# A decoder layer on one core: batches outside heads, every weight part kept on chip, and a batch's later layers woven into the next batch's heads through one PSUM bank

## The chip, the cores and the metric

The kernel runs on one core of a Trainium2 chip. The metric is the device time of one execution in microseconds (us), from start to end; lower is better. Three runs of the kernel before gave 434.12, 434.87 and 435.01 us. The engines are TensorE (PE; its weight loads are listed as PEld), VectorE (DVE), ScalarE (ACT), GpSimd (POOL) and SyncE (SP), which here issues the DMAs. SBUF is the on-chip memory of 128 partitions, PSUM the eight banks (512 fp32 for each partition) that TensorE writes.

## The reference

There are 4 batches of 256 tokens with 256 channels, 16 heads of width 128. In short:

```
# L0_attn: 16 heads, head width 128
q, k, v = x @ Wq, x @ Wk, x @ Wv              # 256 -> 16 x 128 each
q, k = rmsnorm(q) * q_rms_w, rmsnorm(k) * k_rms_w
scores = q k^T / sqrt(128) - slope[h] * distance, causal
y = rmsnorm(softmax(scores) @ v) * subln_w
x = layernorm(x + concat(y) @ Wproj)           # Wproj 2048 x 256
# L0_xattn: attention computed from ctx alone, applied along x's channel axis
a = softmax((ctx Wq'^T + bq)(ctx Wk'^T + bk)^T)
x = layernorm(x + x @ a^T)
# L0_ffn: weights rounded to three levels, activations to 8 bits
h = sigmoid(quant(x) @ quant(Wgate)^T) * (quant(x) @ quant(Wup)^T)
out = layernorm(x + quant(h) @ quant(Wdown)^T)
```

## The kernel before

**Instruction streams.** Every engine runs one list of instructions in order; the lists are written out by hand, with semaphores between them. Nothing reorders them, so an instruction that waits holds back all that stands behind it on its engine.

**Heads first, batches inside.** The attention is 64 *steps*, each one head of one batch. `attention_steps` (L206) runs over heads outside and over the 4 batches inside; eight steps (two heads) make one trip of a hardware loop. The pipeline is deep: in step `n` TensorE projects q, k and v of step `n` (`qkv(0)`, `qkv(1)`, one for each 128 tokens, L470 to L484, six matmuls of 384 columns each), turns the normed q and k of step `n-1` (L493), turns the probabilities of step `n-2` (L499), computes the scores of `n-1` (L505, L506) and the values of `n-2` (L512 to L514), and turns y of `n-3` (L521). The fp32 inputs are split into a high and a low part, and three products of the parts are summed.

**Who does what in a step.** ScalarE takes squares of q and k and copies v (L635, L639), applies the exponential (L644, L645), copies qT, kT and yT (L661, L662, L651) and squares y (L673). VectorE sums the squares (L797, L804), norms q and k (L791) and y (L812), copies the turned probabilities out of PSUM (L817) and adds the bias to the scores with a running extreme (L835). GpSimd computes the reciprocal roots by a power (L310, L315), splits the weights of the next head into parts (L276, L280) and halves the bias (L325). The order that matters below is VectorE's: `norm` of tile 1 of the step before, y's sum, `sums(0)`, y's norm, the copy pT, `norm(0)`, `sums(1)`, the scores.

TensorE may not overwrite q, k, v of a tile until that tile is normed, and may not turn q and k before both tiles are normed:

```
qkv(0)
if live(1):
    for t in range(TT):
        pe.wait_ge(s_qkn[t], n)
    ...
    last.then_inc(s_tqk, 1)
...
qkv(1)
```

**Weights.** Two heads' parts are on chip at a time; SyncE loads the next head while one is used, three DMAs for each. The feed-forward weights are rounded and turned in the last three steps of each trip (`quantise_ff`, `turn_ff`), 24 pieces of 256 columns. The cross attention of all four batches is computed ahead of the heads and in their first steps.

**After the heads.** yT of all 64 steps lies in SBUF. A loop over the 8 tiles of 128 tokens (L535 to L589) runs projection (`project`, L410), first layer norm, cross attention, second norm, gate, up, hidden quantisation, down and last norm. One tile's feed-forward half is woven with the next tile's first half, and the projection matmuls of later tiles (`fill`) stand in TensorE's gaps.

## Time and profile before

| what | value |
|---|---|
| median of three runs | 434.87 us |
| profiled execution: span from first to last instruction | 432.9 us |
| its time around the span, taken as the median less the span | 2.0 us |
| busy: PE, DVE, ACT, POOL | 401.9, 327.7, 254.4, 220.2 us |
| bytes moved | 14.52 MB |

An engine's busy time is the time in which at least one of its instructions runs. The profiled execution's own time is known only as its span; the whole time of a run is taken as the span plus 2.0 us. Clock means the TensorE clock that was granted, with 1.00 for full speed.

### The profile page before, as it was taken

Reading aid. Unit: us, or ns where it says so; the run is one execution under the profiler, and the core shown is the slowest. Engines: PE = TensorE matmul, PEld = TensorE weight load, DVE = VectorE, ACT = ScalarE, POOL = GpSimd, SP = SyncE. Lnnn points to the kernel's source line nnn. Section 1 sums busy time; section 2 is a strip of 40 time slices with the busy share of each in tenths; the row PEclk is TensorE's granted clock in tenths of the full one; section 3 lists DMA queues with packets and bytes.
Section 4 is the critical chain, followed back from the end, with each engine's and each line's share of the span. In section 5 each row is a group of like instructions: output and inputs, shape, how many; then the busy total and the mean of one; then the engine's idle time right before and its main releaser. Section 6 shows DMA issues by size and latency. Waiting matters only on the chain.

```text
span 432.9 us, 9595 instructions
## 1 busy us (share of the span) xinstructions
PE 401.9 (93%) x2605; PEld 361.1 (83%) x2612; DVE 327.7 (76%) x1000; ACT 254.4 (59%) x750; POOL 220.2 (51%) x368
## 2 busy tenths in 40 slices
PE   4979999999999999999999999999999899999552
PEld 3668899999999999999999999999988677777321
DVE  0777987887797798788779779878822788888862
ACT  3486777677676776767767677676722333333321
POOL 3633667676675776767767677675501122222210
PEclk9999999999999999999999999999999999999965
DMA  8980010110101101011010110000000000000000
GB/s 223 316 251 2 2 36 3 38 37 0 36 0 36 36 0 36 0 36 36 0 36 0 36 36 0 0 0 0 0 2 0 2 0 15 12 14 12 13 14 24
DMA packets 21747, 14.52 MB, mean 34 GB/s; under 512 B 1760, under 2 KB 21472, under 8 KB 21728
## 3 DMA queue, kind: packets, MB, share of 16 engines
q1 hardware_dynamic: 21728, 14.29, 11.2%
q8 instruction: 9, 0.15, 0.2%
q14 instruction: 10, 0.08, 0.1%
HBM read 13.24 MB, written 1.05 MB: 33 GB/s over the span
## 4 chain that ended last, share of the span: by engine, by line
PE 86%; DVE 5%; ACT 4%; issue 2%; DMA 1%; POOL 1%; SPq 0%; POOLq 0%; DVEq 0%
PE ps L482 30%; PE ps L422 11%; PE ps L493 7%; PE ps L506 6%; PE ps L499 5%; PE ps L512 4%; PE ps L505 3%; PE ps L514 3%; PE ps L513 3%; PE ps L521 3%; PE ps L587 3%; PE ps L572 2%; ACT hT L696 2%; DMA x_sb<-in_x 1%; PE ps L557 1%
## 5 line engine op out<-in xcount | busy, mean ns | idle before, releaser
L315 POOL TENSOR_TENSOR qk_rstd<-qk_sum,minus_half 128x2 f32<-128x2 f32 x128 | 88.5, 692 | 92.6 <-DVE qk_sum L797 90.8
L482 PE MATMUL ps<-w_hi,xT_hi 128*128 128x384 f32 x256 | 96.9, 378 | 2.3 <-DVE qk_n L791 1.4
L482 PE MATMUL ps<-w_hi,xT_lo 128*128 128x384 f32 x256 | 86.5, 338 | 0.0
L482 PE MATMUL ps<-w_lo,xT_hi 128*128 128x384 f32 x256 | 86.3, 337 | 0.0
L797 DVE TENSOR_REDUCE qk_sum<-sq 128x2 f32<-128x258 f32 x128 | 53.6, 419 | 30.8 <-ACT sq L635 29.1
L635 ACT ACTIVATE sq<-ps 128x256 f32<-128x256 f32 x128 | 49.1, 384 | 34.6 <-PE ps L482 34.4
L791 DVE TENSOR_TENSOR qk_n<-ps,qk_rstd 128x256 f32<-128x256 f32 x128 | 54.2, 423 | 18.8 <-POOL qk_rstd L315 17.8
L422 PE MATMUL ps<-wp,yT 128*128 128x256 f32 x256 | 62.2, 382 | 0.0
L310 POOL TENSOR_TENSOR y_rstd<-y_sum,minus_half 128x2 f32<-128x2 f32 x64 | 49.0, 766 | 24.6 <-DVE y_sum L804 20.9
L673 ACT ACTIVATE sqy<-ps 128x258 f32<-128x258 f32 x64 | 24.8, 387 | 58.5 <-PE ps L514 58.5
L422 PEld LDWEIGHTS ps<-wp,yT 128*128 128x128 f32 x256 | 46.7, 190 | 5.9
L482 PEld LDWEIGHTS ps<-w_hi,xT_hi 128*128 128x128 f32 x256 | 48.4, 189 | 3.0 <-DVE qk_n L791 1.7
L482 PEld LDWEIGHTS ps<-w_lo,xT_hi 128*128 128x128 f32 x256 | 48.6, 190 | 0.0
L482 PEld LDWEIGHTS ps<-w_hi,xT_lo 128*128 128x128 f32 x256 | 48.0, 188 | 0.0
L352 POOL TENSOR_SCALAR var_eps<-mean_var 128x1 f32<-128x1 f32 x24 | 7.0, 292 | 79.6 <-DVE mean_var L846 79.6
L835 DVE CUSTOM_DVE_ANT_0 score<-ps,bias 128x128 f32<-128x128 f32 (+1 forms) x128 | 40.3, 352 | 2.8 <-PE ps L506 2.8
L493 PE MATMUL ps<-ident,qk_n 128*128 128x128 f32 x256 | 38.7, 273 | 0.8 <-DVE qk_n L791 0.6
L506 PE MATMUL ps<-kT,qT 128*128 128x256 f32 x128 | 38.2, 380 | 0.0
L280 POOL TENSOR_TENSOR w_lo<-w_raw,w_hi 128x256 fp32r<-128x256 f32 x48 | 35.4, 738 | 4.0
L817 DVE COPY pT<-ps 128x384 f32<-128x384 f32 x64 | 35.1, 548 | 2.6 <-PE ps L499 2.5
L493 PEld LDWEIGHTS ps<-ident,qk_n 128*128 128x128 f32 x256 | 31.1, 140 | 5.0 <-issue 3.2
L639 ACT COPY v_sb<-ps 128x128 f32<-128x128 f32 x128 | 34.0, 266 | 0.0
(126 smaller groups left out, 846.9 us busy)
## 6 DMA issues: line engine op xcount, KB each, us to landing
w_raw<-in_L_attn_Wq SPq DMA_DIRECT2D x16, 128.0 KB, 2.2
w_raw<-in_L_attn_Wk SPq DMA_DIRECT2D x16, 128.0 KB, 2.3
w_raw<-in_L_attn_Wv SPq DMA_DIRECT2D x16, 128.0 KB, 2.3
wp<-in_L_attn_Wproj SPq DMA_DIRECT2D x1, 2048.0 KB, 16.1
ff_raw<-in_L_ffn_w_gate SPq DMA_DIRECT2D x1, 1024.0 KB, 8.6
ff_raw<-in_L_ffn_w_up SPq DMA_DIRECT2D x1, 1024.0 KB, 11.0
ff_raw<-in_L_ffn_w_down SPq DMA_DIRECT2D x1, 1024.0 KB, 13.0
out<-fin SPq DMA_DIRECT2D x8, 128.0 KB, 1.7
```

Source lines behind the costliest of these rows:

```text
L280: pool.tensor_tensor(lo, raw, hi, ALU.subtract).then_inc(s_split, 1)
L310: pool.tensor_tensor(y_rstd[:], y_sum[:], minus_half[:], ALU.pow).then_inc(s_ry, 1)
L315: pool.tensor_tensor(qk_rstd[:, t, :], qk_sum[:, t, :], minus_half[:], ALU.pow).then_inc(s_rs[t], 1)
L422: last = pe.matmul(ps[:, u % 2, 0:C], yT[:, h * B + b, t * P:(t + 1) * P], wp[:, h, :], start=(h == 0), stop=(h == H - 1))
L482: last = pe.matmul(ps[:, t, 0:3 * D], xa[:, k, tok], wa[:, r, k * 3 * D:(k + 1) * 3 * D], start=(i == 0), stop=(i == len(parts) - 1))
L493: last = pe.transpose(dst[:, t * P:(t + 1) * P], qk_n[:, t, a, :], ident[:])
L506: pe.matmul(ps_s[:, S1], qT[:, P:T], kT[:], start=True, stop=True).then_inc(s_s, 1)
L635: act.activation(sq[:, t, :, 0:D], ps[:, t, 0:2 * D].rearrange("p (a d) -> p a d", a=2), ACT.Square).then_inc(s_sq[t], 1)
L791: dve.tensor_tensor(qk_n[:, t], ps[:, t, 0:2 * D].rearrange("p (a d) -> p a d", a=2), r, ALU.mult).then_inc(s_qkn[t], 1)
L797: dve.tensor_reduce(qk_sum[:, t, :], sq[:, t], AX.X, ALU.add).then_inc(s_ss[t], 1)
L817: dve.tensor_copy(pT[:], ps_pT).then_inc(s_pT, 1)
L835: last = dve.tensor_tensor_reduce(score[:, s], ps_s[:, s], bias[:, r, s], 1.0, 3e38, ALU.add, ALU.min, neg_max[:, t:t + 1])
```

## The change

The kernel is rewritten around a different loop order.

- **Order.** Steps are `n = b * 16 + h`: a batch's 16 heads, then the next batch. The steps are no hardware loop any more but are written out. SBUF holds the high and low parts of all 16 heads (`w_hi`, `w_lo`); `w_lo` lies over the raw weights.
- **Splitting the weights.** `split_hi` is now a VectorE copy of 768 columns at the end of steps 0 to 12 (head `n+3`), and heads 1 and 2 before the first step; GpSimd computes only the low parts, three pieces in each of steps 0 to 13. The loads come in groups of heads (1, 1, 2, 4, 4, 4), six DMAs each.
- **Projection.** Each head is multiplied with `Wproj` in step `n+4` (`project(n - 4)`), accumulated in one bank for the whole batch.
- **Turned probabilities** (pT) are copied by ScalarE instead of VectorE. qT and kT share a bank with the scores, so turning q and k of the next head waits for the scores to be read.
- **Side bank.** All other TensorE work goes through one bank, in two slots a step: slot 0 between turning the probabilities and `qkv(n, 1)`, slot 1 after the values. Each job waits until the job before it has been read.
- **Later layers.** Batches 0 to 2 run their projection's end, both norms, cross attention and feed-forward in the 17 steps of the next batch; batch 3 runs them after the last step, both tiles side by side. The sigmoid is replaced by a tanh, `sigmoid(z) = (1 + tanh(z/2)) / 2`.
- **Feed-forward weights** are quantised in 6 units of 1024 columns, in VectorE's steps 7, 9, 11, 13, 15, 17.

The diff, cut to its core:

```diff
+    for b in range(B):
+        first = b * H + (2 if b == 0 else 1)
+        slots[first, 0] = ("ctx_turn", b)
+        slots[first + 1, 0] = ("ctx_project", b)
+        slots[first + 2, 0] = ("energies", b)
+        slots[first + 3, 1] = ("attn_turn", b)
+        if b < LAST:
+            slots[b * H + (13 if b == 0 else 7), 1] = ("x_turn", b + 1)
+            n = b * H + H
+            slots[n + 5, 1] = ("x1_turn", b)
+            slots[n + 6, 1] = ("cross", b)
+            slots[n + 9, 0] = ("xq_turn", b)
+            for i in range(4):
+                slots[n + 9 + i, 1] = ("gate", b, i)
+                slots[n + 10 + i, 0] = ("up", b, i)
+            slots[n + 14, 0] = ("hq_turn", b, 0)
+            slots[n + 15, 1] = ("hq_turn", b, 1)
+            slots[n + 16, 0] = ("down", b)
+    slots[7, 0] = ("ff_sums",)
+    FF_STEPS = [8, 10, 12, 14, 16, 18]
+    for i, n in enumerate(FF_STEPS):
+        slots[n, 1] = ("ff_turn", i)
...
         @block.sync
+            load_x(0)
+            load_w(0)
+            load_w(1)
+            for n, v in ((0, q_rms), (1, k_rms), (2, subln), (3, xbq), (4, xbk)):
+                sp.dma_start(vecs[:, n:n + 1], v.rearrange("(p a) -> p a", a=1)).then_inc(s_vec, 16)
+            load_w(2)
+            sp.dma_start(xw_sb[:, 0, :], xwq).then_inc(s_xw, 16)
+            sp.dma_start(xw_sb[:, 1, :], xwk).then_inc(s_xw, 16)
+            load_ctx(0)
+            load_wp(0)
+            load_w(3)
+            load_ff(0)
...
         @block.gpsimd
+            for n in range(STEPS + 3):
+                s, b = n % H, n // H - 1
+                if n >= 3:
+                    pool.wait_ge(s_ssy, n - 2)
+                    wait(pool, s_yn, n - 3)
+                    pool.tensor_tensor(y_rstd[:], y_sum[:], minus_half[:], ALU.pow).then_inc(s_ry, 1)
+                if n + 2 < H:
+                    split_lo(n + 2, 0)
+                if n < STEPS:
+                    for t in range(TT):
+                        pool.wait_ge(s_ss[t], n + 1)
+                        wait(pool, s_qkn[t], n)
+                        pool.tensor_tensor(qk_rstd[:, t, :], qk_sum[:, t, :], minus_half[:], ALU.pow).then_inc(s_rs[t], 1)
+                        if n + 2 < H:
+                            split_lo(n + 2, t + 1)
...
         @block.tensor
+            def turn_qk(n):
+                for t in range(TT):
+                    pe.wait_ge(s_qkn[t], n + 1)
+                wait(pe, s_sc, n)
...
+            def project(n):
+                b, h = divmod(n, H)
+                pe.wait_ge(s_yT, n + 1)
...
+                for t in range(TT):
+                    last = pe.matmul(total[:, t * C:(t + 1) * C], yT[:, n % 2, t * P:(t + 1) * P], wp[:, h, :],
+                                     start=(h == 0 and t == 0), stop=(h == H - 1), skip_group_check=True)
+                last.then_inc(s_pr, 1)
...
+            for n in range(STEPS + DEPTH):
+                if n < STEPS:
+                    qkv(n, 0)
+                if 0 <= n - 1 < STEPS:
+                    turn_qk(n - 1)
+                if 0 <= n - 2 < STEPS:
+                    turn_p(n - 2)
...
+                slot(n, 0)
+                if n < STEPS:
+                    qkv(n, 1)
+                if 0 <= n - 1 < STEPS:
+                    scores(n - 1)
+                if 0 <= n - 2 < STEPS:
+                    values(n - 2)
+                slot(n, 1)
+                if 0 <= n - 4:
+                    project(n - 4)
+                if 0 <= n - 3 < STEPS:
+                    turn_y(n - 3)
...
         @block.vector
+            dve.wait_ge(s_w0hi, 1)
+            dve.tensor_tensor(w_lo[:, 0], w_raw[:, 0], w_hi[:, 0].bitcast(F32), ALU.subtract).then_inc(s_w0, 1)
+            x_lo(0, ps[:, 0, :], s_x0)
+            split_hi(1)
+            split_hi(2)
...
+            for n in range(STEPS + DEPTH + 1):
+                s, fb = n % H, n // H - 1
+                if 0 <= n - 1 < STEPS:
+                    norm(n - 1, 1)
+                side_read(n - 1, 1)
...
+                if n < STEPS:
+                    norm(n, 0)
+                side_read(n, 0)
+                for b in range(B):
+                    if slots.get((n, 1)) == ("attn_turn", b):
+                        norm_cross(b)
+                if n + 1 in FF_STEPS:
+                    quantise_ff(FF_STEPS.index(n + 1))
+                if 0 <= fb < LAST:
+                    if s == 4:
+                        take_projection(fb, BOTH)
+                    if s == 5:
+                        norm_x1(fb, BOTH)
+                    if s == 8:
+                        scale_x2(fb, BOTH)
+                    if s == 12:
+                        hidden_scale(fb, 0)
+                    if s == 13:
+                        quantise_hidden(fb, 0)
+                    if s == 14:
+                        hidden_scale(fb, 1)
+                    if s == 15:
+                        quantise_hidden(fb, 1)
...
+                if n < STEPS:
+                    sums(n, 1)
+                if 0 <= n - 1 < STEPS:
...
+                    for t, cols in enumerate((S0, S1)):
+                        last = dve.tensor_tensor_reduce(score[:, cols], ps_s[:, cols], dist[:, cols], slope, 3e38,
+                                                        ALU.add, ALU.min, neg_max[:, t:t + 1])
+                    last.then_inc(s_sc, 1)
+                if n + 3 < H:
+                    split_hi(n + 3)
+                if 0 <= fb < LAST and s == 8:
+                    quantise_x2(fb, BOTH)
+                if n in (4, 5, 6):
...
+            def quantise_ff(unit):
...
+                link(dve.tensor_scalar(raw, raw, w_inv[:, i:i + 1], ROUND, ALU.mult, ALU.add))
+                link(dve.tensor_scalar(raw, raw, -ROUND, 1.0, ALU.add, ALU.min))
...
+                dve.tensor_scalar(quantised, raw, -1.0, None, ALU.max).then_inc(s_wq, 1)
+            def split_hi(h):
+                group = [g for g, (first, end) in enumerate(W_GROUPS) if first <= h < end][0]
+                dve.wait_ge(s_wraw[group], 16 * 3 * KC)
+                dve.tensor_copy(w_hi[:, h], w_raw[:, h]).then_inc(s_whi, 1)
```

## Rows read from the trace of the kernel before

**Rows 1.** Page, busy time of each engine.
```profile
PE 401.9 (93%) x2605; PEld 361.1 (83%) x2612; DVE 327.7 (76%) x1000; ACT 254.4 (59%) x750; POOL 220.2 (51%) x368
```

**Rows 2.** Page, the chain of waits that ended last, by engine.
```profile
PE 86%; DVE 5%; ACT 4%; issue 2%; DMA 1%; POOL 1%; SPq 0%; POOLq 0%; DVEq 0%
```

**Rows 3.** Busy time by stretch (columns: stretch, its length, busy us of PE, PEld, DVE, ACT, POOL, clock, DMA share, GB/s).
```profile
10.00:12.00 2.00, 2.00 (x4) 0.96 (x4) 0.85 (x3) 0.59 (x1) 1.28 (x3) 1.00 1.10 206
...
200.00:300.00 100.00, 100.00 (x703) 96.14 (x702) 81.74 (x266) 70.28 (x231) 67.31 (x105) 1.00 0.06 16
```

**Rows 4.** Timeline of TensorE, one step (columns: start us, length us, engine, line, instruction).
```profile
208.76 0.42 PE L482 MATMUL ps<-w_hi,xT_hi 128*128 128x384 f32 x1
...
209.90 0.60 PE L493 MATMUL ps<-ident,qk_n 128*128 128x128 f32 x4
210.33 0.49 PE L499 MATMUL ps<-ident,prob 128*128 128x128 f32 x3
...
211.72 0.38 PE L505 MATMUL ps<-kT,qT 128*128 128x128 f32 x2
...
213.18 0.42 PE L482 MATMUL ps<-w_hi,xT_hi 128*128 128x384 f32 x1
```

**Rows 5.** Timeline of VectorE, the same step.
```profile
211.81 0.41 DVE L791 TENSOR_TENSOR qk_n<-ps,qk_rstd 128x256 f32<-128x256 f32 x1
212.39 0.42 DVE L797 TENSOR_REDUCE qk_sum<-sq 128x2 f32<-128x258 f32 x1 [0.17 <-ACT sq L635]
...
213.62 0.42 DVE L791 TENSOR_TENSOR qk_n<-ps,qk_rstd 128x256 f32<-128x256 f32 x1 [0.25 <-POOL qk_rstd L315]
```

**Rows 6.** Timeline of TensorE, projection matmuls behind each other at full clock.
```profile
319.87 2.76 PE L422 MATMUL ps<-wp,yT 128*128 128x256 f32 x12
322.46 0.49 PE L499 MATMUL ps<-ident,prob 128*128 128x128 f32 x3
```

**Rows 7.** Groups of instructions by line (columns: instruction, count, busy us, mean ns, idle before).
```profile
L865 DVE SCALAR_TENSOR_TENSOR ff_raw<-ps,gate_up_scale,ff_raw 128x512 f32<-128x512 f32 x16 | 11.9, 747 | 3.2 <-PE ps L587 2.9
...
L845 DVE BATCH_NORM_STATS2 stats<-res 128x6 f32<-128x256 f32 x24 | 10.3, 427 | 0.8
...
L886 DVE TENSOR_REDUCE h_most<-ff_raw 128x1 f32<-128x1024 f32 x8 | 9.8, 1220 | 0.3
...
L895 DVE TENSOR_SCALAR hq<-ff_raw 128x1024 bf16<-128x1024 f32 x8 | 5.5, 683 | 1.4 <-ACT ff_raw L694 1.4
...
L648 ACT ACT_TABLE_LOAD x1 | 1.3, 1283 | 0.0
```

**Rows 8.** Timeline of SyncE's queue, first and fifteenth DMA issue.
```profile
0.73 0.40 SPq L232 DMA_DIRECT2D yT<-in_L_xattn_Wq  x1
...
8.65 0.47 SPq L225 DMA_DIRECT2D w_raw<-in_L_attn_Wv  x1
```

**Rows 9.** Timeline of TensorE, step 2's start, and the scores behind the last qkv.
```profile
27.72 0.45 PE L482 MATMUL ps<-w_hi,xT_hi 128*128 128x384 f32 x1 [0.85 <-ACT yT L618]
...
310.72 0.38 PE L505 MATMUL ps<-kT,qT 128*128 128x128 f32 x2
```

**Rows 10.** Timeline of TensorE in the last two tiles' feed-forward.
```profile
402.74 1.05 PE L572 MATMUL ps<-wdT,hT 128*128 128x256 bf16 x8 [0.62 <-ACT hT L696]
...
405.33 1.03 PE L587 MATMUL ps<-wuT,xqT 128*128 128x512 bf16 x4
```

**Rows 11.** Timeline of all engines, the last tile's feed-forward and its end.
```profile
412.30 0.41 DVE L851 TENSOR_SCALAR x<-res,mean_var,ln_rstd 128x256 f32<-128x256 f32 x1 [0.19 <-POOL ln_rstd L355]
...
413.99 1.89 PE L572 MATMUL ps<-wdT,hT 128*128 128x256 bf16 x8 [1.10 <-ACT hT L696]
...
430.25 0.41 DVE L851 TENSOR_SCALAR fin<-res,mean_var,ln_rstd 128x256 f32<-128x256 f32 x1 [1.02 <-POOL ln_rstd L355]
```

**Rows 12.** Timeline of GpSimd, one small operation alone and under a VectorE copy.
```profile
394.17 0.19 POOL L352 TENSOR_SCALAR var_eps<-mean_var 128x1 f32<-128x1 f32 x1 [3.60 <-DVE mean_var L846]
...
400.26 0.64 POOL L352 TENSOR_SCALAR var_eps<-mean_var 128x1 f32<-128x1 f32 x1 [4.29 <-DVE mean_var L846]
```

More of the change, by code:

```diff
@@ new lines, in _ @@
+            for t in range(TT):
+                pe.wait_ge(s_hq, 2 * LAST + t + 1)
+                for f in range(FC):
+                    last = pe.transpose(bank16(4 * t)[:, f * P:(f + 1) * P], hq[:, t, f * P:(f + 1) * P], ident16[:])
+                last.then_inc(s_th, 1)
+                pe.wait_ge(s_hT, t + 1)
+                for f in range(FC):
+                    last = pe.matmul(ps[:, 4 * t + 1, 0:C], hT[:, t, f, :], wdT[:, f, :],
+                                     start=(f == 0), stop=(f == FC - 1))
+                last.then_inc(s_dn, 1)
@@ L707, in _ @@
+            for t in range(TT):
+                round_hidden(LAST, t)
+                act.wait_ge(s_th, t + 1)
+                act.copy(hT[:, t].rearrange("p f q -> p (f q)"), ps[:, 4 * t, :].bitcast(BF16)).then_inc(s_hT, 1)
         @block.vector
@@ new lines, in quantise_x2 @@
+            def quantise_x2(b, sel):
+                for t in range(sel.start, sel.stop):
+                    last = dve.tensor_scalar(res[:, t], x2[:, t], x_inv[:, t:t + 1], ROUND, ALU.mult, ALU.add)
+                link(last)
+                dve.tensor_scalar(xq[:, sel], res[:, sel], ROUND + 127.0, -ROUND, ALU.min, ALU.add).then_inc(s_xq, 1)
+                for t in range(sel.start, sel.stop):
+                    last = dve.tensor_scalar(gate_up_scale[:, t], w_half[:], x_scale[:, t:t + 1], None, ALU.mult)
+                last.then_inc(s_gus, 1)
@@ new lines, in _ @@
+            for t in range(TT):
+                take_projection(LAST, slice(t, t + 1))
+            for t in range(TT):
+                norm_x1(LAST, slice(t, t + 1))
+            for t in range(TT):
+                dve.wait_ge(s_xm, t + 1)
+                link(dve.tensor_tensor(res[:, t], ps[:, 4 * t + 1, 0:T], x1[:, t], ALU.add))
+                moments(1, LAST, slice(t, t + 1))
+            for t in range(TT):
+                scale_x2(LAST, slice(t, t + 1))
+                quantise_x2(LAST, slice(t, t + 1))
@@ new lines, in _ @@
+            for t in range(TT):
+                for f in range(2):
+                    dve.wait_ge(s_up, 2 * t + f + 1)
+                    dve.wait_ge(s_sig, 2 * t + f + 1)
+                    last = hidden_part(t, f, ps[:, 4 * t + 2 + f, :])
+                link(last)
+                hidden_scale(LAST, t)
+            for t in range(TT):
+                quantise_hidden(LAST, t)
+            for t in range(TT):
+                dve.wait_ge(s_dn, t + 1)
+                link(take_down(LAST, t, ps[:, 4 * t + 1, 0:C]))
+                moments(2, LAST, slice(t, t + 1))
@@ L914 @@
+            dve.wait_ge(s_out, 16 * LAST)
+            for t in range(TT):
+                normed(2, LAST, slice(t, t + 1), fin).then_inc(s_fin, 1)
 _INS = ["x", "ctx_1024", "L0_attn_Wq", "L0_attn_Wk", "L0_attn_Wv", "L0_attn_Wproj", "L0_attn_q_rms_w",
```

1236 lines of the change are left out of this document (600 added, 636 removed).

## The prediction, written before the changed kernel was run

> **What bounds the kernel now.** I read the busy times first: TensorE is busy 401.9 us of a span of 432.9, VectorE 327.7 [rows 1]. Then the chain of waits: 86% of it is TensorE [rows 2]. Then the busy times by stretch: in the heads, from 200 to 300 us, TensorE is busy 100 of 100 us at full clock, VectorE 82, ScalarE 70, GpSimd 67 [rows 3]. So the heads go by TensorE's instructions, and the timeline gives their price: a step without feed-forward work lasts 213.18 - 208.76 = 4.42 us [rows 4]. Inside it, turning q and k starts 1.14 us after the step's first matmul, the second `qkv` is over 2.96 us after it (the start of the scores, 211.72), four fp32 transposes take 0.43 us, 0.11 each [rows 4].
>
> How near VectorE is to holding TensorE up is read in the same step. The second tile's normed q and k are ready at 213.62 + 0.42 = 214.04, 2.32 us after the second `qkv` ended [rows 4, 5]. TensorE wants them when its next step turns q and k, 213.18 + 1.14 = 214.32. The slack is 0.28 us. I carry that number through the change.
>
> **TensorE's work in a step of the changed kernel.** Projection matmuls behind each other take (322.46 - 319.87) / 12 = 0.216 us an instruction [rows 6], and one fp32 matmul is two instructions. `project` puts two matmuls, four instructions, 0.86 us, into each step: 4.42 + 0.86 = 5.28 us. It is the same work that stood behind the heads before, only moved.
>
> The side jobs of one batch, by the same prices (0.43 us for an fp32 matmul of 256 columns, 0.11 for a transpose): turning ctx 0.2, its projection 0.9, energies 0.9, turning the attention 0.4, turning x 0.4: 2.8. Later layers: turning x1 0.4, cross attention four matmuls 1.7, gate and up 16 instructions at 0.22 (four last 1.03 with the last one's own length in it) [rows 10] 3.5, turning xq and hq some 1.1, down 16 at 1.05 / 8 = 0.13 [rows 10] 2.1: 8.8. Inside the steps run four times the first (one x less), three times the second, and the feed-forward weights' turns, some 3: 11 + 26 + 3 = 40 us.
>
> **The start.** SyncE issued its 15th DMA at 8.65 after the first at 0.73, 0.57 us for each [rows 8]. Group 2 (heads 2 and 3) is the 19th to 24th DMA: issued by about 13, landed by about 15. VectorE's `split_hi(2)` stands before the first step and waits for it, and behind it on VectorE stands every norm. So `qkv(1)` starts at about 18 although `qkv(0)` could start at 9. Group 3 (1.6 MB) is the 29th to 34th: some 4.2 MB have to land before its last byte, at 206 GB/s in a stretch of head weights [rows 3] and more for wide rows, so at 20 to 25. `split_hi(4)` ends VectorE's step 1 and waits for it; the norm behind it lets TensorE turn q and k at about 25.5, so step 2 counts as begun at 24.5. Before it began at 27.7 [rows 9]: 3 us gained. If the weights came in time, step 2 would begin at about 16; both ends stay for the range.
>
> From 24.5: 61 steps of 5.28 (322, less 2 for a pipeline not yet full), 40 of side jobs, 3 to the end of the last `qkv`: 387.5 us. Before that point was 310.7 [rows 9].
>
> **VectorE's late work.** This is where TensorE can stop. The projection adds 0.86 us between the second `qkv` and the next turn, so the slack of 0.28 becomes 1.14. In each step VectorE has a place between `norm(n, 0)` and `sums(n, 1)`. What is put there, X, delays the second tile's norm except for the gap before the sums (some 0.2) and TensorE's slot-0 job in that step; what is put behind the scores, Y, delays it beyond a gap of 0.25 that GpSimd's power leaves [rows 5]. Slot-1 jobs add to the slack. TensorE's stop is X - 0.2 + Y - 0.3 - 1.14 less the slots. The waiter is `turn_qk`, and behind it the whole of TensorE's list. The copy pT has left VectorE, but it stood before `norm(n, 0)`, which goes by GpSimd's result, and gives nothing back here.
>
> - Feed-forward quantising: three passes of 1024 columns at 0.68 [rows 7] make X = 2.1; in steps 7 to 12 Y is `split_hi`, 768 columns, 0.55 if it runs at the speed of that row, 0.9 at one column a cycle (the 0.43 of the 256-column rows); near the first. Stops: 1.5, 1.1, 1.1, 0.3, 0.7, 0.5: 5.
> - Steps 4 to 6: a reduction of 1024 columns, 1.22 [rows 7], with `split_hi`: Y = 1.6, and ScalarE's exponentials before its second squares in step 4: 2.3 in all.
> - Step 4 of a batch: norming the attention 0.9, taking the projection (0.75, two statistics of 0.43 [rows 7], some small ones) 1.85: X = 2.7, less 0.44 for the slot: 0.9.
> - Step 8: `scale_x2` 1.9 as X, `quantise_x2` 1.45 as Y: 1.7.
> - Step 12: the up product 0.75, the reduction 1.22 and five small ones: 2.85, less two slots: 0.6. Step 13, where ScalarE's rounding came late: 0.5. Step 14: 0.4.
>
> Together 4.1 us for each of three batches, 12.3, and with the first two 19.6. I take 20; below, 0 is possible if my places are off by more than a microsecond, above, 35 if GpSimd is held up too. For that the trace has a row: the same small GpSimd operation took 0.19 us alone and 0.64 where it ran into a 1024-column VectorE copy [rows 12].
>
> The Trainium skill, page "GPSIMD Engine Reference", "Key points", says that GpSimd shares its SBUF interfaces with VectorE and contends with its 2-port mode; the two rows agree. By that rule the three quantising passes and `split_hi`, both of that kind, would also hold up GpSimd's low parts and powers behind them, and the sum would be some 5 us longer; without it, as above.
>
> End of the last `qkv`: 387.5 + 20 = 407.5.
>
> **The drain.** The last head has nothing beside it. Norm 2.3 us after `qkv` [rows 4, 5], turn and copies 1.4, scores 0.8, bias 0.75, exponentials 0.9, turn and copy 0.95, values 0.75, squares, sum, power and norm 2.2, turn and copy 0.85, projection 0.95: 11.8 at full clock (durations as their neighbours in a step, 0.4 for 256 columns). Down for one tile took 1.05 us at 402.7 and 1.89 at 414.0, after TensorE had stood idle [rows 10, 11]; TensorE's 4 us here would be up to twice as long. I take 13.
>
> **The tail.** Before, the last tile needed 430.66 - 412.30 = 18.4 us from its second norm to its last [rows 11], and 2.2 more for the store. Now the two tiles of batch 3 go side by side. Worked out in order: second tile's x1 normed at 3.7 us, both cross products (PE in order, slow clock) at 7.6, the second norm of tile 0 at 9.2, its gate and up by 14.3, hidden scale 17.1. But `quantise_hidden` of tile 0 stands behind `hidden_scale` of tile 1 on VectorE, which ends at 20.8. Then 0.7, turn 1.0, copy 1.0, and ScalarE rounds tile 1 only now: 24.7; quantise, turn, copy, down 29.4; take, statistics, power, norm 32; store 34. Bounds 30 and 37.
>
> **Sum.** 407.5 + 13 + 34 = 454.5 for the span that was 432.9, and with the 2.0 around it 456.5 for the median that was 434.87. What this measurement can tell from no change is about 0.2%, 0.9 us.
>
> **Rivals.**
> - *TensorE never waits in the steps*: my slack is too small or the extra work falls better. For it: VectorE has, in all, far less to do in a step (pT gone, 5.28 us instead of 4.42). Against: the list is in order and X sits right before the sums. Then 454.5 - 20 + 2 = 436.5.
> - *Faster*: weights arrive ahead of VectorE's two early waits. Step 2 begins 8 us sooner, and it decides from the point where stops take less than 6 us of it. For it: DMA is otherwise quiet. Against: SyncE's 0.57 us an issue [rows 8]. With no stops it gives 428.5.
> - *A convoy*: GpSimd's contention [rows 12], and ScalarE, 70% busy before [rows 3], late in the gate steps, with pT, a tanh and a rounding more in one step. It would be worst if tanh needed another function table than the exponential: two loads for each of the 12 tanhs in the steps, 24 x 1.28 [rows 7] = 31 us, half of it or all on the path: 456.5 + 15 to 31 = 471 to 487. The Trainium skill, "ScalarE: Activation LUTs", "Table sets: the hidden batching unit", has tanh in the set of exp; by that rule no reload, and the case keeps only its GpSimd half. No row of before holds a tanh.
>
> **Chances.** The forecast, with stops of 10 to 28 us (446 to 466), 0.60. No stops, 0.12, a small part of it within 0.2%. Faster 0.18. Convoy 0.10. The range leaves out the upper convoy and the lower half of the faster case: 430 to 470; the likeliest case alone has 446 to 466. Faster 0.18, same 0.04, slower 0.78.
>
> **What the profile after would show.** Right: steps without extra work at 5.28 us; TensorE idle before turning q and k, released by VectorE's norm of the second tile, in steps 4 to 17 and in steps 4, 8, 12 to 14 of each later batch, 15 to 25 us in all; step 2 at about 24; the last `qkv` near 407; 45 us or more from there to the end, at a falling clock. Wrong: no such idle time (then 436.5), first weights before 15 us, or a tail under 30 us. What would break it altogether is a step that isn't 5.28: if the side bank's one-job rule holds TensorE up in the slots, all sums grow.

## The result and the profile after

The changed kernel takes 459.42 us, the median of four runs (458.29 to 460.65), against 434.5 us of the kernel before, run beside it: a ratio of 1.0575, 95% interval 1.0553 to 1.0597. The prediction was 456.5 us, slower, range 430 to 470. The profiled execution has a span of 456.6 us; 454.5 was predicted.

The page of the changed kernel, busy time by engine and the chain of waits. They answer to [rows 1, 2].

```profile
PE 405.7 (89%) x2610; PEld 368.5 (81%) x2620; DVE 288.4 (63%) x902; ACT 285.4 (63%) x797; POOL 180.1 (39%) x283
...
PE 35%; issue 29%; POOL 23%; DVE 5%; SPq 4%; ACT 1%; DMA 1%; POOLq 0%; DVEq 0%; ACTq 0%
```

TensorE has nearly the work that it had (405.7 us for 401.9), VectorE 39 us less, GpSimd 40 less. So 20 of the span's 24 us more are TensorE's idle time, the span less the busy time: 31.0 us before, 50.9 after. The chain seems to say that GpSimd and "issue" took over. It misleads here, and the busy times by stretch show it (columns: stretch, length, busy us of PE, PEld, DVE, ACT, POOL, clock, DMA share, GB/s):

```profile
105.00:200.00 95.00, 91.94 (x605) 85.22 (x607) 61.66 (x194) 65.31 (x189) 33.26 (x50) 1.00 0.02 6
200.00:300.00 100.00, 97.67 (x651) 90.86 (x652) 65.35 (x214) 69.12 (x198) 36.22 (x55) 1.00 0.03 8
400.00:410.00 10.00, 9.55 (x70) 8.56 (x69) 7.06 (x25) 8.18 (x22) 3.45 (x5) 1.00 0.01 2
410.00:420.00 10.00, 7.61 (x49) 6.03 (x47) 4.66 (x16) 3.43 (x9) 2.22 (x4) 1.00 0.07 26
420.00:430.00 10.00, 5.06 (x16) 3.52 (x16) 4.91 (x15) 0.99 (x3) 2.42 (x7) 0.83 0.00 0
430.00:440.00 10.00, 6.34 (x19) 2.34 (x20) 7.52 (x23) 4.09 (x7) 0.73 (x2) 0.66 0.00 0
440.00:457.00 17.00, 5.83 (x32) 3.62 (x32) 7.12 (x18) 3.58 (x4) 1.54 (x4) 0.55 0.05 16
```

Between 200 and 300 us TensorE is busy 97.67 us where it was busy 100 [rows 3]; it is still the bound there, with short stops. Behind 410 us it is busy 24.8 of 47 us, and its clock falls from 1.00 (2.4 GHz) to 0.55, near the lower level of 1.2 GHz. Three places follow: the start, the stops, and what stands behind the last `qkv`.

**The start.** TensorE's timeline (`qkv(1)`, then turning q and k of the second head) and VectorE's.

```profile
18.18 0.66 PE L453 MATMUL ps<-w_hi,xT_hi 128*128 128x384 f32 x1 [6.15 <-DVE qk_n L739]
...
25.81 0.63 PE L463 MATMUL ps<-ident,qk_n 128*128 128x128 f32 x4 [1.47 <-DVE qk_n L739]
```

```profile
14.66 0.56 DVE L857 CAST w_hi<-w_raw 128x768 fp32r<-128x768 f32 x1 [5.61 <-DMA w_raw<-in_L_attn_Wv]
```

VectorE waits 5.61 us for the 24th DMA and only then comes to the sums of the first head (16.37); TensorE waits 6.15 us for the norm. Predicted: data at about 15, `qkv(1)` at 18, the turn at 25.5. SyncE issued that DMA at 11.84, 23 issues after its first at 0.72: 0.48 us for each.

**The steps.** I measured the distance between one turn of q and k and the next in all 64 steps and took off 5.28 us and the slot jobs. A step without jobs, TensorE, and its neighbour that holds `scale_x2` and `quantise_x2`:

```profile
354.39 0.60 PE L463 MATMUL ps<-ident,qk_n 128*128 128x128 f32 x4
...
359.69 0.60 PE L463 MATMUL ps<-ident,qk_n 128*128 128x128 f32 x4
...
366.41 0.63 PE L463 MATMUL ps<-ident,qk_n 128*128 128x128 f32 x4 [1.27 <-issue]
```

5.30 us, and 6.72. The stop of 1.44 us is put down to "issue"; VectorE's timeline of the same step, one batch earlier, says what it is (its turn is at 267.55):

```profile
263.00 0.73 DVE L772 TENSOR_SCALAR ff_raw<-ff_raw,mean_var,ln_rstd 128x256 f32<-128x256 f32 x2
263.76 0.69 DVE L782 TENSOR_REDUCE x_most<-ff_raw 128x2 f32<-128x512 f32 x1
264.48 0.17 DVE L783 TENSOR_SCALAR x_scale<-x_most 128x2 f32<-128x2 f32 x1
264.69 0.17 DVE L784 RECIPROCAL x_inv<-x_scale 128x2 f32<-128x2 f32 x1
264.89 0.42 DVE L745 TENSOR_REDUCE qk_sum<-sq 128x2 f32<-128x258 f32 x1
...
265.78 0.61 DVE L788 TENSOR_SCALAR ff_raw<-ff_raw,x_inv 128x256 f32<-128x256 f32 x2
266.42 0.43 DVE L790 TENSOR_SCALAR ff_raw<-ff_raw 128x512 bf16<-128x512 f32 x1
266.77 0.35 DVE L792 TENSOR_SCALAR gate_up_scale<-w_half,x_scale 128x2 f32<-128x2 f32 x2
267.03 0.42 DVE L739 TENSOR_TENSOR qk_n<-ps,qk_rstd 128x256 f32<-128x256 f32 x1
```

The later layer's work stands ahead of the sums (264.89) and again ahead of the norm of tile 1 (267.03), with no idle time between; TensorE turns q and k 0.1 us after that norm ends. All the stops by place:

| place | predicted us | measured us |
|---|---|---|
| steps 4, 5, 6 (weight sums) | 2.3 | 1.63, 0.78, 0.44 = 2.85 |
| steps 7, 9, 11, 13, 15, 17 (weight codes) | 1.5, 1.1, 1.1, 0.3, 0.7, 0.5 | 1.83, 1.18, 1.18, 0.44, 0.76, 0.54 |
| later batch, step 4 | 0.9 | 0.65 |
| step 8 | 1.7 | 1.45 |
| steps 12, 13, 14 | 0.6, 0.5, 0.4 | 0.64, 0.04, 0.45 |
| all 62 steps | 19.6 | 19 |

The stops of the later batch (steps 4, 8, 12, 13, 14) repeat in batches 1 to 3 within 0.02 us. The remaining 0.5 us of the sum is under 0.1 a step. Not all of them lie before the turn of q and k: in step 5 the side bank's slot holds TensorE, which waits 0.41 us for VectorE there, before it turns the attention (47.63).

**Behind the last `qkv`.** It ends at 405.26 (407.5 predicted). TensorE's timeline from there:

```profile
405.26 0.38 PE L475 MATMUL ps<-kT,qT 128*128 128x128 f32 x2
...
408.16 0.60 PE L463 MATMUL ps<-ident,qk_n 128*128 128x128 f32 x4
...
409.37 1.91 PE L432 MATMUL ps<-wdT,ff_raw 128*128 128x256 bf16 x16
...
420.30 1.13 PE L495 MATMUL ps<-wp,yT 128*128 128x256 f32 x4 [0.56 <-ACT yT L667]
...
425.67 3.04 PE L549 MATMUL ps<-attn,ff_raw 128*128 128x256 f32 x8
...
443.78 1.04 PE L567 MATMUL ps<-ident,hq 128*128 128x128 bf16 x8 [4.34 <-DVE hq L811]
445.92 1.89 PE L571 MATMUL ps<-wdT,ff_raw 128*128 128x256 bf16 x8 [1.10 <-ACT ff_raw L720]
447.79 1.03 PE L567 MATMUL ps<-ident,hq 128*128 128x128 bf16 x8
449.92 1.89 PE L571 MATMUL ps<-wdT,ff_raw 128*128 128x256 bf16 x8 [1.10 <-ACT ff_raw L720]
```

The drain lasts to 421.4: 16.1 us for 13. The down product of batch 2 (409.37) stands in it. The tail lasts 35.2 us for 34, with the wait of 4.34 us for the hidden codes that stand behind the other tile's scale.

### The profile page after: what moved, and what is told of

The parts are those of the page before. It is cut to its first block, busy times and chain, and to the rows that moved or that the text cites. A ratio compares the mean times of both kernels' runs of the same rounds, so it can differ in the third digit from the quotient of the medians.

```text
span 456.6 us, 8725 instructions
## 1 busy us (share of the span) xinstructions
PE 405.7 (89%) x2610; PEld 368.5 (81%) x2620; DVE 288.4 (63%) x902; ACT 285.4 (63%) x797; POOL 180.1 (39%) x283
## 3 DMA queue, kind: packets, MB, share of 16 engines
q1 hardware_dynamic: 21616, 14.29, 10.8%
HBM read 13.24 MB, written 1.05 MB: 31 GB/s over the span
## 4 chain that ended last, share of the span: by engine, by line
PE 35%; issue 29%; POOL 23%; DVE 5%; SPq 4%; ACT 1%; DMA 1%; POOLq 0%; DVEq 0%; ACTq 0%
POOL qk_rstd L338 12%; PE ps L453 11%; PE ps L495 5%; POOL y_rstd L331 5%; POOL w_lo L305 5%; SPq L229 3%; PE ps L463 3%; PE ps L476 2%; PE ps L470 2%; PE ps L482 1%; PE ps L484 1%; PE ps L483 1%; DMA w_raw<-in_L_attn_Wv 1%; PE ps L503 1%; PE ps L432 1%
## 5 line engine op out<-in xcount | busy, mean ns | idle before, releaser
L338 POOL TENSOR_TENSOR qk_rstd<-qk_sum,minus_half 128x2 f32<-128x2 f32 x128 | 92.0, 719 | 164.1 <-DVE qk_sum L745 163.6
L453 PE MATMUL ps<-w_hi,xT_hi 128*128 128x384 f32 x256 | 100.4, 392 | 9.6 <-DVE qk_n L739 6.1
L453 PE MATMUL ps<-w_hi,xT_lo 128*128 128x384 f32 x256 | 87.7, 343 | 0.0
L739 DVE TENSOR_TENSOR qk_n<-ps,qk_rstd 128x256 f32<-128x256 f32 x128 | 54.3, 424 | 46.1 <-POOL qk_rstd L338 45.4
L331 POOL TENSOR_TENSOR y_rstd<-y_sum,minus_half 128x2 f32<-128x2 f32 x64 | 44.1, 689 | 61.9 <-DVE y_sum L906 61.9
L495 PE MATMUL ps<-wp,yT 128*128 128x256 f32 x256 | 66.7, 383 | 1.1 <-ACT yT L667 1.1
L495 PEld LDWEIGHTS ps<-wp,yT 128*128 128x128 f32 x256 | 44.8, 190 | 7.3 <-ACT yT L667 1.6
L951 DVE CUSTOM_DVE_ANT_0 score<-ps,dist 128x128 f32<-128x128 f32 (+1 forms) x128 | 40.1, 351 | 0.0
L661 ACT ACTIVATE prob<-score,neg_max 128x128 f32<-128x128 f32 x64 | 25.5, 398 | 22.0 <-DVE neg_max L951 21.9
L667 ACT ACTIVATE yT<-ps,vecs 128x256 f32<-128x256 f32 x64 | 29.5, 461 | 7.4 <-PE ps L503 7.4
L676 ACT ACTIVATE qT<-ps,q_scale 128x256 f32<-128x256 f32 x64 | 30.8, 481 | 5.1 <-PE ps L463 4.6
```

Source lines behind the costliest of these rows:

```text
L331: pool.tensor_tensor(y_rstd[:], y_sum[:], minus_half[:], ALU.pow).then_inc(s_ry, 1)
L338: pool.tensor_tensor(qk_rstd[:, t, :], qk_sum[:, t, :], minus_half[:], ALU.pow).then_inc(s_rs[t], 1)
L453: last = pe.matmul(ps[:, t, 0:W3], xa[:, b % 2, k, tok], wa[:, h, k * W3:(k + 1) * W3], start=(i == 0), stop=(i == len(parts) - 1))
L495: last = pe.matmul(total[:, t * C:(t + 1) * C], yT[:, n % 2, t * P:(t + 1) * P], wp[:, h, :], start=(h == 0 and t == 0), stop=(h == H - 1) ...
L676: act.activation(qT[:], ps_qT, ACT.Copy, scale=q_scale[:, m % H:m % H + 1])
L739: dve.tensor_tensor(qk_n[:, t], ps[:, t, 0:2 * D].rearrange("p (a d) -> p a d", a=2), r, ALU.mult).then_inc(s_qkn[t], 1)
```

## The experiments

Each of the first five edits one part of the changed kernel and was to give back one term of the sum. Runs were on several chips; the kernel before had medians of 434.2 to 435.5 us beside them. So each has its ratio to the kernel before too, to be held against 1.0575. Beside the five single edits the kernel before took 0.9 to 1.0 us more than beside the changed kernel, so by the ratios each gains 0.9 to 1.5 us more than by the medians below. What an edit did is therefore read from the traces too, by the times of the 64 turns of q and k.

| kernel | median us | ratio, interval | span |
|---|---|---|---|
| changed kernel | 459.42 | 1.0575, 1.0553 to 1.0597 | 456.6 |
| codes over two steps | 455.74 | 1.0469, 1.0448 to 1.0491 | 452.5 |
| later work over more steps | 453.01 | 1.0394, 1.0362 to 1.0426 | 452.0 |
| loads in another order | 454.65 | 1.0444, 1.0421 to 1.0466 | 452.6 |
| tail's codes in another order | 457.01 | 1.0497, 1.0475 to 1.0518 | 454.1 |
| tail kept warm | 455.43 | 1.0449, 1.0417 to 1.0482 | 454.3 |
| pT copied by VectorE | 460.39 | 1.0555, 1.0517 to 1.0594 | 462.3 |
| one extra pass | 458.35 (one run) | | 456.5 |
| three extra passes | 469.26 (one run) | | 467.4 |
| the five together | 439.19 | 1.0116, 1.0085 to 1.0147 | 437.1 |
| and four more | 436.84 | 1.0055, 1.0039 to 1.0071 | 433.6 |
| and six more | 432.03 | 0.9942, 0.9921 to 0.9962 | 430.3 |

### The weight codes over two steps

```diff
-    FF_STEPS = [8, 10, 12, 14, 16, 18]
+    FF_STEPS = [9, 11, 13, 15, 17, 19]
...
-                    quantise_ff(FF_STEPS.index(n + 1))
+                    quantise_ff(FF_STEPS.index(n + 1), False)
+                if n + 2 in FF_STEPS:
+                    quantise_ff(FF_STEPS.index(n + 2), True)
```

The same three passes, one of them a step earlier (the `x_turn` of batch 1 moves a step to make room).

> The quantising of the feed-forward weights is spread: each unit's first pass stands in one step of VectorE, its second and third in the next, and the turns move one step later (x's turn for batch 1 too). No work is added or left out. Placement theory (late work between the norm of tile 0 and the sums of tile 1 stops TensorE by what exceeds the slack): the stops of steps 7, 9, 11, 13, 15 and 17, 5.9 us in the changed kernel's profile, shrink to under 1, and the median goes from 459.4 to about 454.5. Rival (the stops come from the load as such, of VectorE or GpSimd in the weight-splitting steps): the same work gives the same time, 459.4.

Measured 455.74: 3.7 us less, where 4.9 were expected. Waits of TensorE for VectorE's norm of q and k, in the changed kernel and then in this one (columns: us in total, times, longest):

```profile
PE ps L463 <- DVE qk_n L739: 7.3, 8, 1.8
```

```profile
PE ps L463 <- DVE qk_n L739: 3.0, 5, 0.8
```

TensorE's waits before this turn that are put down to "issue" hardly changed (7.4 and 8.5 us). By the distances of the turns the steps take 2.9 us less: about half of the 5.9 us of stops is left, and not under 1 us as expected. It lies mostly in steps 8, 10 and 12, 0.8 to 1.0 us each, which now hold two passes and a split of weights. Same instructions, half of these stops: what costs is how the work lies to the slack of each step, not its amount.

### Later layers' VectorE work over more steps

```diff
-                        take_projection(fb, BOTH)
+                        take_projection(fb, BOTH, False)
...
-                    if s == 8:
-                        scale_x2(fb, BOTH)
...
-                if 0 <= fb < LAST and s == 8:
-                    quantise_x2(fb, BOTH)
+                if 0 <= fb < LAST:
+                    if s == 4:
+                        moments(0, fb, BOTH)
+                    if s == 7:
+                        scale_x2(fb, BOTH)
+                    if s == 8:
+                        quantise_x2(fb, BOTH)
+                    if s == 11:
+                        dve.wait_ge(s_side_out, JOB["up", fb, 1] + 1)
+                        hidden_most(0)
```

The turned attention of batches 1 to 3 and the turned x move by three steps and one step.

> Inside batches 1 to 3 VectorE's late work is spread, none left out: the attention's norm goes from step 4 to step 7, the first norm's statistics to the end of step 4, the second norm and x2's scale from the middle of step 8 to the end of step 7, the hidden row's reduction of tile 0 from step 12 to the end of step 11. Placement theory: the stops of steps 4, 8 and 12 (0.65, 1.45, 0.64 us in each of three batches, 8.2 in all) shrink to about 0.2 together: some 7.5 us less, 452. Rival (load, not place): 459.4. If the places behind the scores cost as much as those before the sums, half of it: 455.5.

Measured 453.01: 6.4 us less. The stops at steps 4, 8 and 12 are gone (the turn that was at 267.55 comes 5.74 us after the one before it, 0.02 over its jobs); step 7 has a new one of 0.55 us, for it now holds the attention's norm and the cross attention's residual, and step 13 one of 0.33.

```profile
259.46 0.63 PE L463 MATMUL ps<-ident,qk_n 128*128 128x128 f32 x4 [0.28 <-issue]
265.20 0.60 PE L463 MATMUL ps<-ident,qk_n 128*128 128x128 f32 x4
```

From step 20 on the trace is 5.8 us shorter; 7.5 were expected. The same trace shows a cost of long stops that the sum did not have. Behind step 7's stop the clock fell (the turn, then TensorE's busy time by stretch with the clock as the third number from the end):

```profile
63.18 0.95 PE L463 MATMUL ps<-ident,qk_n 128*128 128x128 f32 x4 [1.84 <-DVE qk_n L739]
```

```profile
64.00:66.00 2.00, 2.00 (x9) 2.00 (x8) 0.89 (x3) 1.12 (x3) 2.00 (x4) 0.50 0.00 0
```

The next turn comes 7.40 us after this one, where it is 5.80 in the changed kernel's trace, with the same stop and the clock at 1.00. The traces of two more kernels below, the warm tail and pT on VectorE, have the same 1.6 us there. Why the clock fell in some executions and not in others stays open.

### The loads

Heads 2 and 3 get loads of their own, a load with a head of its own takes 3 DMAs instead of 6, and the cross attention's inputs go behind head 3.

```diff
-    W_GROUPS = ((0, 1), (1, 2), (2, 4), (4, 8), (8, 12), (12, 16))
+    W_GROUPS = ((0, 1), (1, 2), (2, 3), (3, 4), (4, 6), (6, 8), (8, 12), (12, 16))
...
```

> Heads 0 to 3 are loaded one by one with three DMAs each instead of six, ahead of the cross attention's inputs; heads 4 to 7 in two groups. Theory (VectorE's two early waits for weights hold back every norm, and SyncE's issue rate makes the weights late): turning q and k of head 1 comes at 19 instead of 25.8 us, and everything behind it 6 to 7 us earlier: about 453. Rival (the bytes bound it, 206 to 350 GB/s): under 2 us gained.

Measured 454.65: 4.8 us less. VectorE's split of head 2 (14.66 before), and TensorE's turn of the second head (25.81 before):

```profile
10.68 0.56 DVE L866 CAST w_hi<-w_raw 128x768 fp32r<-128x768 f32 x1 [1.45 <-DMA w_raw<-in_L_attn_Wv]
```

```profile
21.67 0.63 PE L471 MATMUL ps<-ident,qk_n 128*128 128x128 f32 x4 [0.83 <-DVE qk_n L747]
```

4.1 us of the start; the rival, bytes as the bound, had under 2. It came out 2.7 us later than the 19 that I had expected: behind the split at 10.68 it is the chain of the first steps through ScalarE, VectorE and GpSimd that TensorE waits for, no longer a DMA.

### The order of the hidden codes in the tail

```diff
                 link(last)
+                if t == 1:
+                    quantise_hidden(LAST, 0)
                 hidden_scale(LAST, t)
-            for t in range(TT):
-                quantise_hidden(LAST, t)
+            quantise_hidden(LAST, 1)
```

> In the tail VectorE quantises tile 0's hidden row right behind tile 1's two products, ahead of tile 1's reduction and scales. Theory (the tail is one chain of in-order waits, and tile 0's quantising stands behind tile 1's scale): tile 0's turn starts some 2 us earlier, tile 1's last rounding too: 457.4. Rival (tile 1's own chain is the end and TensorE's clock sets it): no change, 459.4.

Measured 457.01: 2.4 us less; from the last projection's end to the end of the span 32.5 us for 35.2. TensorE waits 2.32 us where it waited 4.34:

```profile
442.15 0.62 PE L567 MATMUL ps<-ident,hq 128*128 128x128 bf16 x8 [2.32 <-DVE hq L811]
```

### The tail kept warm

TensorE runs matmuls into a free bank, which nobody reads, where it would stand idle before its turns and its down products; nothing else changes. The first of five places:

```diff
+            def warm(count, bank):
+                for _ in range(count):
+                    pe.matmul(ps[:, bank, :], ident16[:], wuT[:, 0, 0:BANK], start=True, stop=True)
...
             for t in range(TT):
+                warm((11, 2)[t], 3)
                 pe.wait_ge(s_x1, tiles_done(LAST, t))
```

> 45 matmuls of 512 columns whose results nobody reads stand in TensorE's waits of the tail; the computation is complete. Theory (the tail pays for a fallen clock): the cross products, gate, turns and down matmuls of the tail run at 2.4 GHz, 4 us less, 455.4. Rival (the tail goes by VectorE's and ScalarE's chain alone): 459.4, or more, if a spare matmul is in the way.

Measured 455.43: 4.0 us less. The tail by stretch, and its cross products and last down product:

```profile
420.00:430.00 10.00, 8.51 (x39) 5.18 (x40) 4.47 (x13) 1.57 (x4) 2.22 (x6) 1.00 0.00 0
430.00:440.00 10.00, 9.22 (x45) 3.80 (x43) 9.08 (x28) 4.51 (x7) 1.41 (x4) 1.00 0.01 2
440.00:455.00 15.00, 7.23 (x44) 3.84 (x42) 6.33 (x16) 3.16 (x3) 1.54 (x4) 0.84 0.05 17
```

```profile
427.49 1.89 PE L554 MATMUL ps<-attn,ff_raw 128*128 128x256 f32 x8
...
448.53 1.05 PE L581 MATMUL ps<-wdT,ff_raw 128*128 128x256 bf16 x8 [0.24 <-ACT ff_raw L730]
```

The granted clock stayed at 1.00 (2.4 GHz) up to 440 us; the cross products took 1.89 us for 3.04, down 1.05 for 1.89. From the last projection's end to the end of the span: 30.9 us for 35.2. The span is only 2.3 us shorter, for this trace has the 1.6 us behind step 7's stop and a start 0.5 us later. So the clock is a cause of the long tail, shown.

### pT back on VectorE

```diff
+                if 0 <= n - 2 < STEPS:
+                    dve.wait_ge(s_tp, n - 1)
+                    wait(dve, s_y, n - 2)
+                    dve.tensor_copy(pT[:], ps_pT).then_inc(s_pT, 1)
                 if n < STEPS:
                     norm(n, 0)
```

> The copy of the turned probabilities goes back from ScalarE to VectorE, at its old place ahead of the norm of tile 0: 64 x 0.55 = 35 us of VectorE work more. Placement theory: it stands where VectorE waits for GpSimd's power anyway, so within 1 us of 459.4. Rival (VectorE's load makes the stops): each of the some 19 steps with a stop gets up to 0.5 us longer, about 469. A third way, ScalarE was the late one: the time falls by several us.

Measured 460.39 (458.52 to 464.1), no difference from 459.42 that the runs can tell. 64 copies of 0.547 us are 35 us of VectorE's time, and they come out of its idle time before the norm:

```profile
L734 DVE TENSOR_TENSOR qk_n<-ps,qk_rstd 128x256 f32<-128x256 f32 x128 | 54.2, 424 | 18.6 <-POOL qk_rstd L338 17.6
```

That idle time was 46.1 us before the copies. The profiled execution is the slowest of the four (span 462.3), but its copies do not make it so: the last turn of q and k comes 2.5 us later than in the changed kernel, 1.6 of it behind step 7's stop and 0.4 at the start, and another 3.1 us lie in the drain, where the clock fell to 0.50 from 420 us on. Taking pT off VectorE gave nothing back that the runs can tell, as the prediction had it.

### One and three extra passes in VectorE's slack

In steps 2, 6 and 7 of batches 2 and 3 (steps 34 to 55), VectorE reduces 1024 columns, 1.21 us, once or three times, between `norm(n, 0)` and `sums(n, 1)`; nobody reads the result. The edit with three:

```diff
+                if n >= 24 and s in (2, 6, 7):
+                    for k in range(3):
+                        dve.tensor_reduce(w_sum[:, k:k + 1], wp[:, 0:4].rearrange("p h c -> p (h c)"), AX.X, ALU.add)
```

> One reduction of 1024 columns (1.2 us, its result not used) is added in VectorE's place between the norm of tile 0 and the sums of tile 1 in six steps that have no other work there (steps 2, 6 and 7 of batches 2 and 3). Slack theory: 1.2 less 0.2 is under the slack of 1.14, so the distances between the turns of q and k in these steps stay within 0.1 us each. Rival (VectorE's work adds to the step): up to 6 x 1.2 = 7 us.

> The same with three reductions, about 3.5 us in each of the six steps. Slack theory: 3.5 - 0.2 - 1.14 less the slots' TensorE work: 1.3 us more in each step 2, 0.4 in each step 6, 1.7 in step 7 of batch 2 and 2.2 in step 7 of batch 3: 7.3 us in all. If every added us stops TensorE: 21.

One pass: span 456.5 for 456.6, no stop in any of the six steps above 0.04 us. Three passes: the span grows by 10.8 us, where 7.3 was expected. Steps 2 grew by 1.14 and steps 6 by 0.27 (expected 1.3 and 0.4), but steps 7 by 3.1 and 3.5, and the steps 8 behind them by 0.4 and 0.2. VectorE's timeline shows why:

```profile
256.57 0.68 DVE L839 TENSOR_TENSOR ff_raw<-ps,ff_raw 128x512 f32<-128x512 f32 x1
257.29 0.75 DVE L754 BATCH_NORM_STATS2 stats<-ff_raw 128x6 f32<-128x256 f32 x2
258.07 0.25 DVE L757 BATCH_NORM_AGGREGATE mean_var<-stats 128x2 f32<-128x6 f32 x2
...
260.08 0.42 DVE L739 TENSOR_TENSOR qk_n<-ps,qk_rstd 128x256 f32<-128x256 f32 x1 [0.23 <-POOL qk_rstd L338]
260.42 3.46 DVE L923 TENSOR_REDUCE w_sum<-wp 128x1 f32<-128x1024 f32 x3
```

Step 6's late passes and the cross attention's residual (256.57 to 258.3) use up the slack of step 7 before its own passes begin: `norm(n, 0)` starts 3.3 us after the step's turn of q and k (256.75), where it is 1.8 in the changed kernel, and the stop is 1.4 us above the expected 1.7. My expectation had given each edit a slack of its own; there is one in a step, for all that lies in it. The slack itself held: in step 2, where nothing else lies, three passes of 3.46 us less 0.2, the slack of 1.14 and the slot's 0.86 give a stop of 1.26, and 1.14 was measured.

### The edits together, and a faster version

The first five together:

> The five edits that the single runs have timed, together: the feed-forward weights' codes over two steps each, the weights loaded in another order and in fewer transfers, the last batch's hidden codes in another order, a later layer's VectorE work over more steps, and TensorE kept busy with matmuls whose results nobody reads before its turns in the tail. Alone they gave 3.7, 4.8, 2.4, 6.4 and 4.0 us against 459.4. Theory, that each works at a place of its own (steps 6 to 19, the start, the tail, steps 20 to 63, the tail's clock): the sum, 21.3 us, so 438.1 us, with an interval of some 1.5 us either side, and the stops of the 64 steps, 19 us in the changed kernel, down to about 10. Rival, that they lean on the same waits (the order of the hidden codes and the warm clock both act on the last down product, and VectorE's spread work fills slack that the later weight codes of batch 0 need): 442 us or more.

Measured 439.19 us, 438.1 expected. By the ratios the five gave 6.2 hundredths alone and 4.6 together, so the medians' agreement is no proof by itself; the traces decide. In them the start gained 4.4 us (4.1 alone), the steps 8.7 (2.9 alone, and 5.8 without the 1.6 us behind step 7's stop) and the part behind the last turn of q and k 6.4 (2.7 and 4.3 alone): the terms add up but for 0.6 us that the two edits of the tail share. Of the 19 us of stops about 10 are left, as expected. With four more, read from that trace's places:

> The former with what the trace still shows on the path. GpSimd raises the norms' power before it writes the low weight pieces, since in the weight-splitting steps the norm of tile 0 came 0.5 us late behind a piece: 8 steps, about 3 us. Five of the six sums of the feed-forward weights go to ScalarE and VectorE keeps one: about 1 us at steps 4 to 6. VectorE's split of head 2 stands behind the first sums and not ahead of them: about 1 us at the start. The down product of batch 2 stands two steps later, outside the drain of the last heads: 2 us. Theory, that these are on the path: some 7 us less than the kernel with five edits, so 431 us, 0.8% under the kernel before. Rival, that ScalarE, with two more sums of 128x1536 inputs in steps 3 to 7, takes the place of VectorE there and that the drain waits for its chain of softmax and not for the product: 436 us, the same as before within 0.3%.

436.84 us: 2.4 us less, 7 expected; here the rival was right. In the traces the start gained 0.5 us and the steps lost 3.1 us of stops, though step 4 kept one of 1.16 us, ScalarE's sum of step 3 standing ahead of its exponentials. But from the last turn of q and k to the end it was 42.0 us and is 42.1: the down product two steps later took 1.0 us out of the drain and put 1.1 into the tail, for now VectorE's norm of batch 2 stood ahead of the last projection's taking, which began at 404.92 although the projection had ended at 403.7. The profiled execution took 435.46 us, one of the fastest three of twelve. Then six more, each at a stop that this trace showed:

```diff
-                if n in (3, 4, 5, 6, 7):
-                    half = n - 2
+                if n in (4, 5, 6, 7, 8):
+                    half = n - 3
...
+                    if s == 13:
+                        dve.wait_ge(s_side_out, JOB["up", fb, 3] + 1)
+                        hidden_most(1)
...
-                        last = take_down(b, t, side[:, t * C:(t + 1) * C])
+                        last = take_down(b, t, side[:, t * C:(t + 1) * C], (res, fin)[b == LAST - 1])
```

> The former again with what its own trace shows: the reduction of the second hidden tile (1.21 us) behind the scores of the step before; the attention weights of the cross-attention divided by their sums one step earlier, away from the step with the cross-attention's residual; ScalarE's five sums one step later, off the step in which it waits for the energies; VectorE's split of a head's weights behind the sums of tile 0 instead of ahead of the norm of tile 1; in the drain the last head's y turned before the projection of the one before it; batch 2's result kept in its own buffer, so that the last batch's projection is taken before it is normed. Stops in the trace at these places: 0.45 and 0.56 us in each of three batches, 1.16 at step 4, 0.62 and 0.44 at steps 9 and 11, 0.7 and 1.3 in drain and tail, in all 7 us. Theory, that each is on the path and slack is per step: 5 to 7 us less than the former's 436.8, so 431 us, 0.8% under the kernel before. Rival, that the work lands on steps as full as those it leaves: 435 us, no difference from the kernel before.

432.03 us, ratio 0.9942, interval 0.9921 to 0.9962: 0.6% faster than the kernel before, 27 us under the changed kernel. Its page and two stretches:

```profile
PE 408.5 (95%) x2671; PEld 369.7 (86%) x2671; DVE 285.0 (66%) x900; ACT 286.7 (67%) x801; POOL 180.9 (42%) x283
...
PE 82%; DVE 5%; issue 4%; POOL 3%; ACT 3%; SPq 1%; DMA 1%; POOLq 0%; ACTq 0%; DVEq 0%
```

```profile
200.00:300.00 100.00, 99.40 (x661) 92.72 (x660) 67.08 (x223) 69.47 (x199) 36.40 (x55) 1.00 0.03 8
400.00:431.00 31.00, 22.56 (x123) 11.52 (x121) 21.55 (x62) 8.90 (x13) 5.64 (x14) 0.94 0.05 18
```

Not every one of the six was free: the second tile's reduction behind the scores of step 13 took most of step 14's stop of 0.45 away and made step 13's 1.0 where it was 0.33; steps 13 to 15 together take 0.5 us more in each batch. The attention's norm one step earlier took away 0.5 us in each of three batches, and behind the last turn of q and k the trace is 2.0 us shorter. Since six edits ran together, only their places in the trace tell them apart, not a run for each.

## Why the prediction was right, step by step

- **Which engine bounds.** TensorE in the steps, with 5.28 us a step: 5.30 in a step without jobs. Right.
- **The start.** Turn at 25.5, measured 25.81, by the wait that was named. The loads experiment moved it and the time by 4.1 and 4.8 us. Right; shown. One reading was off: the row of the kernel before that is called SyncE's 15th DMA is its 16th, since one of the rows ahead of it holds two, so an issue takes 0.53 us there and not 0.57; the 24th came at 11.84, not 13, and its data at 14.6.
- **The stops.** 19.6 us from one slack of 0.28 + 0.86 = 1.14, measured 19, each place within 0.6 us; in step 13 of a batch, 0.5 us was given to a late rounding on ScalarE, and it was in time. The weight codes were under-sized by 0.7 in sum, 0.33 of it in step 7, which alone holds four small operations of VectorE on the weights' scales (58.83 to 59.51, 0.68 us). In steps 2 to 12 GpSimd's second power, that of tile 1, took 0.98 us instead of 0.69 while VectorE split weights, and a weight piece stands ahead of its first (57.07 in step 7); how much of the error these make is not shown. The weight sums of steps 4 to 6 were under-sized by 0.55, and 0.5 in the other steps was not counted; the later batches were over-sized by 2.6 us. That these errors cancel to 0.6 us is luck. The place of each stop is not: the two spreading experiments (3.7 and 6.4 us) show the cause of both groups.
- **The end of the last `qkv`.** 407.5, measured 405.26. The down product of batch 2 was counted in the steps (2.1 us), but its slot lies behind the last `qkv`; the stops were 0.6 less and the start 0.3 later.
- **The drain.** 13, measured 16.1. This is mostly that same product, mis-placed: 1.75 us of TensorE's time at 409.37, ahead of the last scores, and VectorE's take of it, which lasts to 413.2; only then does the bias of the last scores begin, although they were done at 411.9. In the last version, with the product two steps later and the last y turned ahead of a projection, it is 11.4 us from the last turn of q and k to the last projection's end where it was 13.3; the other 1.2 of the 3.1 us stay open. That TensorE would be slow here was wrong in this execution: the clock stayed at 1.00 up to 420 us. In the run with pT on VectorE it did fall there, and the same stretch took 16.4 us.
- **The tail.** 34, measured 35.2; the order that was worked out is the one in the trace (tile 1's scale done at 20.8, measured 21.6 after the last projection; down done 29.4, measured 30.4). The order of the codes and the clock are shown as causes, 2.4 and 4.0 us; they overlap by 0.6 us.
- **The rivals.** That TensorE never waits fell by the stops, and so did the faster case: all stops and all of the start would have had to go. The convoy of GpSimd is there in small (0.98 for 0.69 us), and the 5 us more that the prediction worked out for it did not come: in step 7 GpSimd's last weight piece ended at 59.15, before VectorE's three passes began at 59.51, so there was nothing for them to hold up; in step 9 they met for 0.3 us, and it was VectorE's pass that took 0.86 us for 0.75. Of its other half, the table loads, the groups by line have one row, below that of the steps' tanhs:

```profile
L628 ACT ACTIVATE ff_raw<-ps,gate_up_scale 128x512 f32<-128x512 f32 x12 | 8.3, 688 | 1.5 <-PE ps L422 0.4
...
L650 ACT ACT_TABLE_LOAD x1 | 1.3, 1283 | 0.7 <-PEq L1002 0.7
```

One table load in the whole run, with 12 tanhs between exponentials: no reload, as the Trainium skill's "ScalarE: Activation LUTs" ("Table sets: the hidden batching unit") has it.

The median lay 2.9 us above the forecast: 2.1 in the span of the profiled execution and 0.8 between that execution (458.4) and the median. The 2.1 are a difference too: 3.1 and 1.2 more in drain and tail, against 2.2 less up to the last `qkv`.

## What to carry to other kernels

An engine that is idle a third of the time can still stop the bound engine, when its list is in order and the work comes in lumps: write down the slack of one step, lay every lump that stands ahead of the awaited instruction into it, and count a step's lumps together. Moving lumps to other steps was worth more here (10 us from two edits) than taking 35 us of copies off the same engine (nothing). Where work leaves the end of a kernel for the steps before it, look at what is left there: here the end without its filling ran by latency, and the bound engine's clock fell with it.
